# Keys of the second cross attention turned once: a store on GpSimd in the first one, two steps moved to ScalarE in the second

## The chip, the core and the metric

The kernel runs on one core of a Trainium2 chip. TensorE multiplies and transposes (a transpose is a product with the identity), VectorE and ScalarE work elementwise from PSUM and SBUF, GpSimd from SBUF alone, and SyncE issues transfers between DRAM and SBUF. GpSimd can issue transfers too. The engines run their own instruction streams and wait for one another on semaphores. The metric is the device time of one execution in microseconds (us), lower is better.

## The reference, cut to what matters

A block of two layers on `x` (16 batches, 64 tokens, 512 features). Each layer is cross attention to a context of 16 x 512 x 512, then a second attention or time mixing, then a feed forward network. Both layers attend to the same context:

```python
x = x + _L0_xattn_ref(_layernorm(x), ctx_1024, ctx_1024, mask, Wq, bq, Wk, bk, Wv, bv, Wo, bo)
...
x = x + _L1_xattn_ref(_layernorm(x), ctx_1024, ctx_1024)
...
def _L1_xattn_ref(query, key, value):          # 16 heads of 32 features, 512 keys
    scores = jnp.einsum('bhqd,bhkd->bhqk', Q, K) / jnp.sqrt(32)
    weights = jax.nn.softmax(scores, axis=-1)
    out = jnp.einsum('bhqk,bhkd->bhqd', weights, V)
```

The first one projects keys and values from the context; the second takes the context as it is. The last feed forward network rounds its weights to three values: `round(w * scale)` clipped to -1 and 1.

## The kernel before, in words

The whole block is one program of stages with barriers between them: layer norm, projected cross attention (`projected_attention`, names `l0x_`), time mixing, a network with 4-bit weights, layer norm, `ternary_means`, the second cross attention (`cross_attention`, names `l1x_`), sparse attention, the ternary network. In each stage every engine has a written-out instruction list; nothing else orders the work.

**First cross attention.** It goes over pairs of batches, 8 steps a pair (4 a batch). For each batch the context (512 keys by 512 features) is loaded and its four feature chunks are turned on TensorE (`turn`, L460), one chunk a step, two batches ahead. A turned chunk is split into an upper and a lower part, so that projections in the faster format lose nothing: VectorE masks the bits into `l0x_upper` (L697) and subtracts (L700, into `l0x_ctxT_lower`), ScalarE copies the upper part into `l0x_ctxT` (L617) and counts `ctxt_ready`. Both are double buffered by batch. TensorE projects with three products a chunk (L478), in two work banks by turns: before it reuses a bank it waits until this bank's last content was copied away, by ScalarE for keys (L621), by VectorE for values (L687, `l0x_V`). VectorE also masks scores (L709), quantises weights of a later stage (L156 to L173, five operations a step in six of eight steps), and sums magnitudes of the ternary weights (L756, and L759, a sum of two 128x1 operands in SBUF). GpSimd subtracts for two weights (L449) and adds the bias row to eight tiles of `X` (L453), and is then done.

**Second cross attention.** 64 steps `k`, four a batch; a step covers two pairs of heads. TensorE's list in a step: turn two probability tiles (L943), in step 2 turn the finished heads of the batch before (L970), scores for step k + 2 (L932), in steps 0 and 2 a half product of probabilities and context (L959), and turn one context chunk for five steps ahead (`turn`, L919). The keys `l1x_KT` are these turned chunks, copied by ScalarE (`key_copy`, L1000) into two buffers. VectorE takes maxima of the scores (L1043) and copies turned probabilities from PSUM (L1071); ScalarE takes exponentials (L1006), copies one of the eight probability tiles of a batch (in step 3, L1026) and the heads (L1012). The first turn of a step waits for the first exponential and for the copy that empties its bank, the second turn for the second ones.

Beside it the ternary weights are rounded in 24 pieces of 128x1024, three a pair of batches, by three passes on GpSimd: scale and add a large number (L886), clip (L889), subtract the number and write bfloat16 (L893). SyncE waits for the third pass, stores the piece and loads the next one, then loads a context once a half product has released its buffer. SyncE's list is in order, so a wait holds what stands behind it.

## Time and profile before

| | us |
|---|---|
| median of 3 runs (1753.8 to 1759.28) | 1757.63 |
| the profiled execution | 1758.54 |
| its span | 1756.8 |

| engine | busy us | share of the span |
|---|---|---|
| TensorE, matmuls | 1528.7 | 87% |
| VectorE | 1122.2 | 64% |
| ScalarE | 591.7 | 34% |
| GpSimd | 295.8 | 17% |

The first cross attention lies at about 51 to 664 us of the span, the second at 1254 to 1461. In the rows below a line of the timeline is start, duration, engine, source line, operation, output and inputs, count; in brackets the idle time of the engine ahead of it and who ended it. PE is TensorE, PEld its weight loads, DVE VectorE, ACT ScalarE, POOL GpSimd, SPq SyncE's queue. The duration of a line with a count spans all of them. Ends of matmuls are modelled; starts are better taken from one line to the next.

### The profile page before, as it was taken

To read this page: it belongs to the slowest core of one execution; us is meant where nothing else is said; L and a number is where in the kernel's file an instruction comes from. 1 tells how busy PE (TensorE), PEld (TensorE's weight loads), DVE (VectorE), ACT (ScalarE), POOL (GpSimd) and SP (SyncE) were. 2 spreads that over 40 slices of the span, in tenths; PEclk is the share of its full clock that TensorE was granted. 3 is DMA by queue.
4 is the path that set the end of the run, shared out by engine and by line. 5 is a ranking of instruction groups with operands and counts; after the bars stand their busy time and mean duration, and the time that the engine had idled before them with its cause. 6 is when DMAs were issued, how large, how long until landed. Compare 5 with 4: busy or idle time off the path is not lost. (4 is left out here: it accounts for less than half of the span.)

```text
span 1756.8 us, 34069 instructions
## 1 busy us (share of the span) xinstructions
PE 1528.7 (87%) x14116; PEld 996.4 (57%) x14130; DVE 1122.2 (64%) x2155; ACT 591.7 (34%) x1221; POOL 295.8 (17%) x185
## 2 busy tenths in 40 slices
PE   6789999999999994998577899998799995895786
PEld 3567777777777763344545344444466663585343
DVE  3257667676676765521975757675488883765575
ACT  1244443443434442132023110111466662044332
POOL 0400000000000000310010000000499992160000
PEclk9889999999999997899888899998899997998899
DMA  6113122231222204000005000000455421004001
GB/s 231 61 39 132 64 84 86 75 126 70 83 80 90 75 19 158 0 0 1 4 2 198 1 0 0 0 0 0 186 178 191 169 99 35 1 3 145 0 0 48
DMA packets 47909, 120.05 MB, mean 68 GB/s; under 512 B 10605, under 2 KB 15469, under 8 KB 43674
## 3 DMA queue, kind: packets, MB, share of 16 engines
q1 hardware_dynamic: 47770, 118.04, 19.6%
q8 instruction: 107, 1.75, 0.4%
q14 instruction: 32, 0.26, 0.0%
HBM read 100.95 MB, written 17.07 MB: 67 GB/s over the span
## 5 line engine op out<-in xcount | busy, mean ns | idle before, releaser
L1130 POOL TENSOR_TENSOR tm_mixed<-tm_mixed,XNT 128x512 f32<-128x512 f32 x16 | 21.8, 1382 | 662.1 <-DVE tm_mixed L1153 662.1
L617 ACT ACTIVATE l0x_ctxT<-l0x_upper 128x512 fp32r<-128x512 f32 x64 | 40.4, 631 | 237.4 <-DVE l0x_ctxT_lower L700 237.4
L478 PE MATMUL bank<-l0x_ctxT,l0x_upper_k 128*128 128x512 f32 x256 | 104.7, 409 | 5.1 <-ACT l0x_upper_k L627 5.1
L697 DVE TENSOR_SCALAR l0x_upper<-bank 128x512 int32<-128x512 int32 x64 | 44.0, 688 | 95.2 <-PE bank L460 90.6
L478 PE MATMUL bank<-l0x_upper_v,l0x_ctxT 128*128 128x512 f32 x256 | 102.6, 401 | 0.0
L478 PE MATMUL bank<-l0x_ctxT,l0x_lower_k 128*128 128x512 f32 x256 | 101.5, 396 | 0.0
L478 PE MATMUL bank<-l0x_ctxT_lower,l0x_upper_k 128*128 128x512 f32 x256 | 101.4, 396 | 0.0
L478 PE MATMUL bank<-l0x_upper_v,l0x_ctxT_lower 128*128 128x512 f32 x256 | 100.6, 393 | 0.0
L478 PE MATMUL bank<-l0x_lower_v,l0x_ctxT 128*128 128x512 f32 x256 | 100.5, 392 | 0.0
L709 DVE CUSTOM_DVE_ANT_0 l0x_prob<-bank,l0x_mask 128x512 f32<-128x512 f32 x128 | 83.1, 687 | 21.2 <-PE bank L489 20.9
L1043 DVE TENSOR_REDUCE l1x_negmax<-bank 128x1 f32<-128x512 f32 x128 | 82.4, 686 | 21.2 <-PE bank L932 20.8
L635 ACT ACTIVATE l0x_prob<-l0x_prob,l0x_negmax 128x512 f32<-128x512 f32 x128 | 91.3, 720 | 3.3 <-DVE l0x_negmax L709 3.3
L687 DVE TENSOR_TENSOR l0x_V<-bank,rows 128x512 f32<-128x512 f32 x64 | 44.1, 689 | 71.7 <-PE bank L478 70.7
L889 POOL TENSOR_SCALAR l1x_piece<-l1x_piece 128x1024 f32<-128x1024 f32 x24 | 87.2, 3634 | 2.0
L1006 ACT ACTIVATE l1x_prob<-bank,l1x_negmax 128x512 f32<-128x512 f32 x128 | 87.1, 689 | 1.3 <-DVE l1x_negmax L1043 1.3
L245 PE MATMUL bank<-ident,XN 128*128 128x128 f32 x192 | 34.4, 363 | 56.4 <-DVE XN L225 56.4
L1627 PE MATMUL bank<-f_gateT,f_x 128*128 128x512 f32 (+1 forms) x192 | 82.3, 572 | 1.4 <-ACT f_x L1665 1.4
L1071 DVE COPY l1x_PT<-bank 128x512 f32<-128x512 f32 x112 | 72.8, 685 | 12.5 <-PE bank L943 12.5
L669 ACT ACTIVATE l0x_PT<-bank 128x512 f32<-128x512 f32 x128 | 69.5, 592 | 33.2 <-PE bank L587 32.1
L1673 ACT ACTIVATE f_silu<-bank 128x512 f32<-128x512 f32 (+1 forms) x24 | 13.5, 562 | 196.7 <-PE bank L1627 196.7
L1651 PE MATMUL bank<-f_downT,f_hT 128*128 128x512 f32 x176 | 78.6, 603 | 1.2 <-ACT f_hT L1683 1.2
L1627 PE MATMUL bank<-f_upT,f_x 128*128 128x512 f32 (+1 forms) x192 | 79.5, 557 | 0.0
(264 smaller groups left out, 3373.5 us busy)
## 6 DMA issues: line engine op xcount, KB each, us to landing
l0x_ctx<-in_ctx SPq DMA_DIRECT2D x16, 1024.0 KB, 5.3
l1x_ctx<-in_ctx SPq DMA_DIRECT2D x16, 1024.0 KB, 5.8
fp_weight<-l0x_weight_piece SPq DMA_DIRECT2D x24, 352.0 KB, 2.4
f_raw<-fp_weight SPq DMA_DIRECT2D x3, 2816.0 KB, 17.4
ternary_weight<-l1x_piece_out SPq DMA_DIRECT2D x24, 256.0 KB, 6.1
f_raw<-ternary_weight SPq DMA_DIRECT2D x3, 2048.0 KB, 14.1
l0x_abs_piece<-in_L_ffn_w_gate SPq DMA_DIRECT2D x8, 512.0 KB, 5.7
l0x_mask<-mask_scratch SPq DMA_DIRECT2D x16, 256.0 KB, 3.6
```

The lines of the kernel that those rows point to most:

```text
L478: last = nc.tensor.matmul(work[bank][:, :], stationary, moving, start=kc == 0 and i == 0, stop=kc == CH - 1 and i == 2)
L635: nc.scalar.activation(prob[:, :], prob[:, :], ACT.Exp, scale=-1.0, bias=w.negmax[:, p:p + 1], accum_out=w.rowsum[:, par, p:p + 1]).then_i ...
L669: nc.scalar.activation(w.PT[r][:, :], probt[i][:, :], ACT.Copy).then_inc(probt_ready, 1)
L687: nc.vector.tensor_tensor(w.V[par][:, p - CH, :], work[bank][:, :], g.rows[:, 0, :], ALU.add).then_inc(value_ready, 1)
L697: nc.vector.tensor_scalar(upper.bitcast(I32), work[bank][:, :].bitcast(I32), UPPER_BITS, None, ALU.bitwise_and).then_inc(ctx_upper, 1)
L709: nc.vector.tensor_tensor_reduce(w.prob[2 * (s % 2) + i][:, :], score[i][:, :], w.mask[par][:, :], 1.0, 3e38, ALU.add, ALU.min, w.negmax[: ...
L889: nc.gpsimd.tensor_scalar(part, part, WHOLE - 1, WHOLE + 1, ALU.max, ALU.min).then_inc(piece_step, 1)
L1006: nc.scalar.activation(w.prob[2 * (k % 2) + i][:, :], score[2 * (k % 2) + i][:, :], ACT.Exp, bias=w.negmax[:, p:p + 1], accum_out=w.rowsum ...
L1043: nc.vector.tensor_reduce(w.negmax[:, p:p + 1], score[2 * (k % 2) + i][:, :], AX.X, ALU.max, negate=True).then_inc(max_ready, 1)
L1071: nc.vector.tensor_copy(w.PT[2 * s + i][:, :], probt[i][:, :]).then_inc(probt_ready[i], 1)
L1627: last = nc.tensor.matmul(bank[:, 0:n], w.x[:, kc, :], weight[:, kc, at:at + n], start=kc == 0, stop=kc == CH - 1)
L1651: ins = nc.tensor.matmul(work[1][:, :], w.hT[:, kc * P:(kc + 1) * P], w.downT[:, kc, :], start=kc == 0, stop=kc == IC0 - 1)
```

## The change

- In the first cross attention GpSimd adds the upper and the lower part of each turned chunk into one buffer `l0x_whole` and stores it (256 KB) to a new DRAM tensor `turned_context`, 64 times, issuing the stores itself and waiting for each before the next addition. VectorE waits, ahead of splitting a chunk into a buffer in use, for the sum of the chunk that was there 8 chunks ago (`whole_ready`). The bias additions stand between the chunks of each pair of batches.
- In the second cross attention TensorE turns no context and ScalarE copies no keys. SyncE loads the keys, 1 MB a batch, into three buffers `l1x_KT` (three of them ahead of the stage, among the context loads), each released by the last scores of its batch.
- The third rounding pass is done by ScalarE (`whole_weights`, with a constant of minus the large number as bias), in steps 2 and 3 of a batch.
- ScalarE copies one probability tile in step 1 too; VectorE one less.

```diff
@@ projected_attention, gpsimd
+            def store_contexts(b):
+                for c in range(CH):
+                    n = b * CH + c
+                    pool.wait_ge(ctxt_ready, n + 1)
+                    if n > 0:
+                        pool.wait_ge(whole_stored, 16 * n)
+                    nc.gpsimd.tensor_tensor(w.whole[:, :], w.ctxT[b % 2][:, c, :].bitcast(F32),
+                                            w.ctxT_lower[b % 2][:, c, :].bitcast(F32), ALU.add).then_inc(whole_ready, 1)
+                    pool.wait_ge(whole_ready, n + 1)
+                    nc.gpsimd.dma_start(d.ctxT[b, :, c, :], w.whole[:, :]).then_inc(whole_stored, 16)
...
                 nc.gpsimd.tensor_tensor(g.X[:, t, :], g.X[:, t, :], g.rows[:, 1, :], ALU.add).then_inc(bias_added, 1)
+                store_contexts(2 * t)
+                store_contexts(2 * t + 1)
+            pool.wait_ge(whole_stored, 16 * B * CH)
@@ vector, context_parts
+                if count > 2 * CH:
+
+                    dve.wait_ge(whole_ready, count - 2 * CH)
@@ cross_attention, sync
+                if b + 3 < B:
+                    sp.wait_ge(score_full, DOUBLES * (b + 1))
+                    sp.dma_start(w.KT[b % 3][:, :, :], d.ctxT[b + 3]).then_inc(keys_loaded[b % 3], 16)
@@ gpsimd, rounding
-                nc.gpsimd.tensor_scalar(w.piece_out[k][:, :], part, WHOLE, None, ALU.subtract).then_inc(piece_done, 1)
@@ tensor
-                if k + AHEAD < B * CH:
-                    turn(k + AHEAD)
@@ scalar
+            def whole_weights(b, k):
+                turn = b // 4
+                act.wait_ge(piece_step, (turn * 6 + k) * 2 + 2)
...
+                nc.scalar.activation(w.piece_out[k][:, :], w.piece[k][:, :], ACT.Identity,
+                                     bias=w.minus_whole[:, :]).then_inc(piece_done, 1)
...
-                if s == 3:
+                if s % 2 == 1:
                     act.wait_ge(probt_full[1], k + 1)
                     if b > 0:
-                        act.wait_ge(half_full, 2 * b)
+                        act.wait_ge(half_full, 2 * b + s // 2 - 1)
                     nc.scalar.activation(w.PT[2 * s + 1][:, :], probt[1][:, :], ACT.Copy).then_inc(probt_ready[1], 1)
                 if k + 1 < STEPS:
                     exponential(k + 1, 1)
-                if k + AHEAD < B * CH:
-                    key_copy(k + AHEAD)
...
+                if s >= 2 and s - 2 < len(PIECES_OF[b % 4]):
+                    whole_weights(b, PIECES_OF[b % 4][s - 2])
@@ vector
-                for i in range(1 if s == 3 else 2):
+                for i in range(1 if s % 2 == 1 else 2):
```

TensorE in the second cross attention, steps 0 to 2 of the first batch, before (`l1x_ctx` is the context, `l1x_prob` a probability tile):

```order
L943 MATMUL bank<-ident,l1x_prob_10781 128x128 x4
L943 MATMUL bank<-ident,l1x_prob_10782 128x128 x4
L932 MATMUL bank<-l1x_KT_10775,XNT 64x512 x4
L919 MATMUL bank<-ident,l1x_ctx_10778 128x128 x4
L943 MATMUL bank<-ident,l1x_prob_10783 128x128 x4
L943 MATMUL bank<-ident,l1x_prob_10784 128x128 x4
L932 MATMUL bank<-l1x_KT_10775,XNT 64x512 x4
L919 MATMUL bank<-ident,l1x_ctx_10778 128x128 x4
```

and the same place now:

```order
L942 MATMUL bank<-ident,l1x_prob_11160 128x128 x4
L942 MATMUL bank<-ident,l1x_prob_11161 128x128 x4
L931 MATMUL bank<-l1x_KT_11152,XNT 64x512 x4
L942 MATMUL bank<-ident,l1x_prob_11162 128x128 x4
L942 MATMUL bank<-ident,l1x_prob_11163 128x128 x4
L931 MATMUL bank<-l1x_KT_11152,XNT 64x512 x4
```

The turns of the context are gone, and scores are followed by the next turn of probabilities directly.

ScalarE in the second cross attention, steps 2 and 3 of the first batch, before (`l1x_PT` is a turned probability tile):

```order
L1006 ACTIVATE l1x_prob_10783,l1x_rowsum<-bank,l1x_negmax 128x512
L1006 ACTIVATE l1x_prob_10784,l1x_rowsum<-bank,l1x_negmax 128x512
L1000 ACTIVATE l1x_KT_10776<-bank 128x512
L1006 ACTIVATE l1x_prob_10781,l1x_rowsum<-bank,l1x_negmax 128x512
L1026 ACTIVATE l1x_PT_10792<-bank 128x512
L1006 ACTIVATE l1x_prob_10782,l1x_rowsum<-bank,l1x_negmax 128x512
L1000 ACTIVATE l1x_KT_10775<-bank 128x512
```

and steps 2 and 3 of the second batch now:

```order
L1007 ACTIVATE l1x_prob_11162,l1x_rowsum<-bank,l1x_negmax 128x512
L1007 ACTIVATE l1x_prob_11163,l1x_rowsum<-bank,l1x_negmax 128x512
L1000 ACTIVATE l1x_piece_out_11187<-l1x_piece_11181,l1x_minus_whole 128x1024
L1007 ACTIVATE l1x_prob_11160,l1x_rowsum<-bank,l1x_negmax 128x512
L1025 ACTIVATE l1x_PT_11171<-bank 128x512
L1007 ACTIVATE l1x_prob_11161,l1x_rowsum<-bank,l1x_negmax 128x512
L1000 ACTIVATE l1x_piece_out_11188<-l1x_piece_11182,l1x_minus_whole 128x1024
```

Passes of 1024 columns stand where key copies of 512 stood; a batch has one or two of them in place of four key copies.

GpSimd in the first cross attention now, behind its two subtractions (before, eight bias additions stood in a row and nothing behind them):

```order
L464 TENSOR_TENSOR X<-X,rows 128x512
L452 TENSOR_TENSOR l0x_whole<-l0x_ctxT_84,l0x_ctxT_lower_105 128x512
L455 DMA turned_context<-l0x_whole 128x512
L452 TENSOR_TENSOR l0x_whole<-l0x_ctxT_84,l0x_ctxT_lower_105 128x512
L455 DMA turned_context<-l0x_whole 128x512
```

Addition and store alternate, eight of each behind every bias addition.

## Rows read from the trace of the kernel before

**Rows 1.** Windows: a stretch of either stage; busy (count) by engine, PEclk, DMA share, GB/s

```profile
400.00:500.00 100.00, 98.56 (x820) 74.34 (x819) 69.06 (x137) 40.56 (x87) 0.00 (x0) 1.00 0.22 71
...
1275.50:1448.10 172.60, 172.55 (x2940) 112.56 (x2936) 146.95 (x253) 118.98 (x310) 168.73 (x71) 1.00 0.47 162
```

**Rows 2.** Timeline, TensorE, one step of the second cross attention

```profile
1276.26 1.10 PE L959 MATMUL bank<-l1x_PT,l1x_ctx 128*32 128x64 f32 x64
1277.29 0.66 PE L919 MATMUL bank<-ident,l1x_ctx 128*128 128x128 f32 x4
1277.78 1.04 PE L943 MATMUL bank<-ident,l1x_prob 128*128 128x128 f32 x8
1278.75 1.09 PE L932 MATMUL bank<-l1x_KT,XNT 32*64 32x512 f32 x8
```

**Rows 3.** Timeline, TensorE, half products 14 batches apart

```profile
1270.27 1.10 PE L959 MATMUL bank<-l1x_PT,l1x_ctx 128*32 128x64 f32 x64
...
1442.80 1.10 PE L959 MATMUL bank<-l1x_PT,l1x_ctx 128*32 128x64 f32 x64
```

**Rows 4.** Timeline, the last steps of the stage, which have no turn of context

```profile
1449.68 1.09 PE L943 MATMUL bank<-ident,l1x_prob 128*128 128x128 f32 x8
...
1450.70 1.09 PE L932 MATMUL bank<-l1x_KT,XNT 32*64 32x512 f32 x8
...
1451.72 1.09 PE L943 MATMUL bank<-ident,l1x_prob 128*128 128x128 f32 x8
1451.86 1.29 DVE L1043 TENSOR_REDUCE l1x_negmax<-bank 128x1 f32<-128x512 f32 x2 [0.20 <-PE bank L932]
...
1452.59 0.69 ACT L1006 ACTIVATE l1x_prob<-bank,l1x_negmax 128x512 f32<-128x512 f32 x1 [1.05 <-DVE l1x_negmax L1043]
```

**Rows 5.** Timeline, VectorE from the maxima of step 1 to those of step 2

```profile
1353.84 1.29 DVE L1043 TENSOR_REDUCE l1x_negmax<-bank 128x1 f32<-128x512 f32 x2 [0.20 <-PE bank L932]
...
1357.48 1.29 DVE L1043 TENSOR_REDUCE l1x_negmax<-bank 128x1 f32<-128x512 f32 x2
```

**Rows 6.** Timeline, the copy between two exponentials, and TensorE's wait behind it

```profile
1445.73 0.60 ACT L1026 ACTIVATE l1x_PT<-bank 128x512 f32<-128x512 f32 x1
1446.20 0.70 ACT L1006 ACTIVATE l1x_prob<-bank,l1x_negmax 128x512 f32<-128x512 f32 x1
...
1447.04 0.42 PEld L943 LDWEIGHTS bank<-ident,l1x_prob 128*128 128x128 f32 x4 [0.27 <-ACT l1x_prob L1006]
```

**Rows 7.** Groups by line: ScalarE's copy of 128x1024; busy us, mean ns, idle before

```profile
L2207 ACT ACTIVATE f_hT<-bank 128x1024 bf16<-128x1024 bf16 x16 | 15.5, 1021 | 5.1 <-PE bank L2173 5.1
```

**Rows 8.** Timeline, TensorE at the start of the second cross attention

```profile
1254.48 2.37 PE L919 MATMUL bank<-ident,l1x_ctx 128*128 128x128 f32 x20 [0.73 <-PEq L2002]
```

**Rows 9.** Timeline, time mixing: VectorE additions without and with GpSimd's beside them

```profile
714.58 0.69 DVE L1160 TENSOR_TENSOR tm_mixed<-tm_mixed,XNT 128x512 f32<-128x512 f32 x1
...
716.67 2.94 POOL L1130 TENSOR_TENSOR tm_mixed<-tm_mixed,XNT 128x512 f32<-128x512 f32 x2 [640.59 <-DVE tm_mixed L1153]
717.17 1.32 DVE L1160 TENSOR_TENSOR tm_mixed<-tm_mixed,XNT 128x512 f32<-128x512 f32 x1
```

**Rows 10.** Bias additions; ScalarE's chunk copies (ns, starts); a store's landing, 1444 to 1462

```profile
66.03 10.04 POOL L453 TENSOR_TENSOR X<-X,rows 128x512 f32<-128x512 f32 x8
...
L617 ACT ACTIVATE l0x_ctxT<-l0x_upper x64: 629/632/634, 53.8 to 610.2; 128x512 fp32r<-128x512 f32 x64
...
ternary_weight<-l1x_piece_out SPq DMA_DIRECT2D x1, 256.0 KB, 4.1
```

**Rows 11.** Timeline, a step of the first cross attention in which TensorE waits

```profile
298.76 0.63 ACT L617 ACTIVATE l0x_ctxT<-l0x_upper 128x512 fp32r<-128x512 f32 x1 [1.20 <-DVE l0x_ctxT_lower L700]
...
299.89 0.16 DVE L759 TENSOR_TENSOR abs_sum<-abs_sum,l0x_abs_part 128x1 f32<-128x1 f32 x1
...
305.01 1.52 DVE L687 TENSOR_TENSOR l0x_V<-bank,rows 128x512 f32<-128x512 f32 x2
...
305.75 0.42 PEld L460 LDWEIGHTS bank<-ident,l0x_ctx 128*128 128x128 f32 x4 [0.37 <-DVE l0x_V L687]
```

More of the change, by code:

```diff
@@ L820, in context_loads @@
     for b in range(len(w.ctx)):
+        if b < 3:
+            sp.dma_start(w.KT[b][:, :, :], d.ctxT[b]).then_inc(w.keys_loaded[b], 16)
         sp.dma_start(w.ctx[b][:, :, :], context(d)[b]).then_inc(w.ctx_loaded[b], 16)
@@ L850, in cross_attention @@
     ctx_dram = context(d)
-    AHEAD = CH + 1
-    turn_bank = [work, pv, probt[0], probt[1]]
-    def chunk_bank(j):
-        return turn_bank[j] if j < CH else work
     with nc.Block() as block:
@@ L889, in rounding @@
                 nc.gpsimd.tensor_scalar(part, part, WHOLE - 1, WHOLE + 1, ALU.max, ALU.min).then_inc(piece_step, 1)
-                pool.wait_ge(piece_step, before + 2)
-                if turn > 0:
-                    pool.wait_ge(piece_stored[k], 16 * turn)
-                nc.gpsimd.tensor_scalar(w.piece_out[k][:, :], part, WHOLE, None, ALU.subtract).then_inc(piece_done, 1)
             def add_heads(t):
@@ L908, in _ @@
         def _(pe):
-            def turn(j):
-                b, c = j // CH, j % CH
-                if c == 0:
-                    pe.wait_ge(ctx_loaded[b % 4], 16 * (b // 4 + 1))
-                if j >= CH:
-                    pe.wait_ge(key_ready, 1 if j == CH else j)
-                if (j - AHEAD) % DOUBLES == 2 and j > AHEAD + DOUBLES:
-                    pe.wait_ge(heads_done, (j - AHEAD) // DOUBLES)
-                for kc in range(KC):
-                    last = nc.tensor.transpose(chunk_bank(j)[:, kc * P:(kc + 1) * P], w.ctx[b % 4][:, kc, c * P:(c + 1) * P],
-                                               g.ident[:, :])
-                last.then_inc(ctx_turned, 1)
             def scores(k):
@@ L926, in scores @@
                 half = s // 2
-                pe.wait_ge(key_ready, b * CH + 2 * half + 2)
+                if s == 0:
+                    pe.wait_ge(keys_loaded[b % 3], 16 * (b // 3 + 1))
                 for e in range(2):
@@ L932, in scores @@
                         last = nc.tensor.matmul(score[2 * (k % 2) + i][e * T:(e + 1) * T, :], w.QT[rows, c, b * T:(b + 1) * T],
-                                                w.KT[b % 2][rows, c, :], start=True, stop=True)
+                                                w.KT[b % 3][rows, c, :], start=True, stop=True)
                 last.then_inc(score_full, 1)
@@ L972, in turn_back @@
                 last.then_inc(heads_back, 1)
-            for j in range(AHEAD):
-                turn(j)
             for k in range(2):
                 scores(k)
-            pe.wait_ge(key_ready, CH)
             for k in range(STEPS):
@@ L985, in _ @@
                     scores(k + 2)
+                if s == 0:
+                    pe.wait_ge(ctx_loaded[b % 4], 16 * (b // 4 + 1))
                 if s == 2:
@@ L1012, in heads_copy @@
                 nc.scalar.activation(w.headsT[b % 2][:, :], pv[:, 0:256], ACT.Copy).then_inc(heads_out, 1)
-            for j in range(AHEAD):
-                key_copy(j)
             for i in range(2):
@@ L2308, in projected_attention_buffers @@
         w.headsT = a("l0x_headsT", [P, CH, P], F32)
+        w.whole = a("l0x_whole", [P, KEYS], F32)
         w.Wq, w.Wk, w.Wv, w.Wo = (a(f"l0x_{n}", [P, CH, D], F32) for n in ('Wq', 'Wk', 'Wv', 'Wo'))
@@ L2338, in attention_buffers @@
         w.QT = g.XNT
-        w.KT = [a(f"l1x_KT{i}", [P, CH, KEYS], F32) for i in range(2)]
+        w.KT = [a(f"l1x_KT{i}", [P, CH, KEYS], F32) for i in range(3)]
+        w.minus_whole = a("l1x_minus_whole", [P, 1], F32)
         w.ctx = [a(f"l1x_ctx{i}", [P, KC, D], F32) for i in range(4)]
@@ L2349, in attention_buffers @@
         w.piece_out = [a(f"l1x_piece_out{i}", [P, ABS_PIECE], BF16, 2) for i in range(6)]
-        w.ctx_loaded, w.piece_loaded = take("ctx_loaded", 4), take("piece_loaded", 6)
+        w.ctx_loaded, w.piece_loaded, w.keys_loaded = take("ctx_loaded", 4), take("piece_loaded", 6), take("keys_loaded", 3)
         return w
```

19 lines of the change are left out of this document (11 added, 8 removed).

## The prediction, made before the run

> **What bounds the kernel now.** I read the busy table by stage first, then the merged timeline of each stage that the change touches, then the groups by line. Both touched stages are bound by TensorE: in the first cross attention it is busy 98.56 of 100 us, with VectorE at 69 and GpSimd at 0; in the steady part of the second it is busy 172.55 of 172.60 us at full clock, with GpSimd at 168.73, VectorE at 146.95 and ScalarE at 118.98 [rows 1]. So what counts is what TensorE loses in the second stage, which engine is next when it does, and what new work on GpSimd does to TensorE in the first stage.
>
> A busy figure of matmuls is modelled, so I take intervals from one start to the next. In a step of the second stage (two pairs of heads; four steps are a batch) the turn of a context chunk takes 0.49, the turn of the probabilities 0.97, a half product, in every second step, 1.03 [rows 2], and the scores 1.02 [rows 4]. From the half product at 1270.27 to the one at 1442.80 there are 14 batches, so a batch takes 12.32 [rows 3]. Four times 2.48 and twice 1.03 leave 0.34, the turn of the finished heads, which is one more short operation of each batch: there is no gap, and TensorE sets the pace.
>
> **The change part by part, second stage.** The change takes out all 64 turns (59 of them between the steps, 5 ahead of them) and the 64 ScalarE key copies. The price of a step without a turn is in the trace, since the last steps of the stage have none: probabilities at 1449.68, scores at 1450.70, probabilities at 1451.72, so 2.04 in place of 2.48 [rows 4]. A turn is thus worth 0.44, not 0.49. The floor of a batch is 4 x 2.04 + 2 x 1.03 + 0.34 = 10.56, a gain of 1.76.
>
> What is late next? I walk one batch, counted from the start of TensorE's step 0, with scores of step 1 at 4.09 (2.04 + 1.03 + 1.02). VectorE can start the maxima 1.16 after the scores start (1450.70 to 1451.86) [rows 4], at 5.25. From there its work of steps 1, 2 and 3 runs without a break: maxima, two copies, reciprocal and heads take 3.64 from 1353.84 to 1357.48 [rows 5], so the next maxima start at 8.89, and take 1.29 until 10.18. Then comes the one copy of step 3 that is left to it, about 0.69, to 10.87. The next batch's first turn of probabilities would like to start at 10.56 and needs the bank that this copy empties: 0.3 late. ScalarE is a little later. Its first exponential for that turn starts 0.73 after the maxima (1451.86 to 1452.59) [rows 4], at 9.62; then, by the new order, the probability copy at 10.31, the second exponential 0.47 behind it at 10.78, and TensorE's second half 0.84 behind that (1446.20 to 1447.04), at 11.62 [rows 6]. The second half begins 0.5 after the first, so the batch turns over at about 11.1. The trace has that very wait once already, 0.27 at 1447.04, where the turn is gone and the copy stands between the exponentials [rows 6].
>
> I take 11.1 a batch, with 10.56 and 12.3 as ends: 14 x (12.32 - 11.1) = **17.1 less**.
>
> The third rounding pass moves from GpSimd to ScalarE, 24 times. For 128x1024 to bfloat16 ScalarE's nearest row is 1.02 [rows 7]. In step 2 it runs from 7.3 to 8.3 in my walk, before the exponential at 9.62 can start: hidden, with 1.3 to spare. In every second batch one more runs in step 3, from 11.5 to 12.5; the exponential behind it then starts 0.8 late, but TensorE wants it only at 14.2 and has it by 14.0: just hidden. If that cover goes, it costs up to 1.5 x 1.02 a batch. GpSimd drops from 98% busy to some 60%, and would otherwise be the bound: its work of 168.73 us in those 172.60 would hold a batch near 12.0. With the pass gone it runs ahead and nobody waits for it, except that the queue of SyncE now waits for ScalarE's pass before it stores a piece.
>
> The one more probability copy (step 1) is 0.60 on ScalarE instead of 0.68 on VectorE; it is in the walk. The key loads are 16 transfers of 1 MB. They stand in SyncE's queue behind the wait for the piece's pass and ahead of the context load; they are issued in step 3 of a batch and wanted in step 2 two batches on, about 19 us, against 5 to 8 that a 1 MB transfer takes. The transfers moved 162 GB/s at a share of 0.47 [rows 1], so 345 at most; a batch will move 3.3 MB in 11.1 us, 295 GB/s. They fit, with little room.
>
> At the start the five turns ahead of the first scores go, 2.37 of TensorE [rows 8], and three turns ahead of the steady part, 1.3: **3.7 less**. Three more megabytes ahead of the weight pieces bring the first piece to GpSimd some 5 us later; ScalarE asks for it in step 2, by then about ready. The stage's last store is now issued about a microsecond after the last probability copy, while half product, heads and the last addition still follow; it lands up to 4.1 later [rows 10]: nothing, or half a us.
>
> **First stage.** GpSimd gets 64 additions of 128x512 and 64 stores of 256 KB, and waits for each store before the next addition. The addition takes 1.25 alone (10.04 / 8) [rows 10] and 1.47 beside VectorE's (2.94 / 2) [rows 9]. A store issued by GpSimd isn't in the trace; SyncE's of 256 KB into DRAM landed after 4.1 in a quiet stretch [rows 10]. So a chunk takes about 5.7; bounds 3.3 (half the landing) and 9.7 (twice it). Chunks come every (610.2 - 53.8) / 63 = 8.8 us [rows 10], so GpSimd keeps up, and VectorE's new wait (for the sum of 8 chunks ago, ahead of a chunk's splitting) never holds. The Trainium skill, page "DMA: Bandwidth & Descriptors", the anatomy of a GpSimd DMA, gives 2.0 us plus the bytes at 436 GB/s, an estimate of 2.6 us here, by which the cycle would be 4.2; no run here shows it yet, and the sum would be the same.
>
> The additions do touch VectorE. Where a GpSimd addition runs at 716.67, VectorE's addition of two SBUF tensors takes 1.32 in place of 0.69, and GpSimd's two take 2.94 in place of 2.5 [rows 9]: one waits for the other. The Trainium skill, page "SBUF — State Buffer", section "Who interferes with whom", says just that: the pair of ports is locked for a whole instruction when a VectorE instruction with two SBUF inputs meets a GpSimd one that reads SBUF. The trace agrees, and the rule speaks against this change.
>
> Where does it reach TensorE? In one place of each pair of batches. At 299.4, when the chunk is ready (298.76 + 0.63), GpSimd's addition would start and run to 300.8; VectorE's tiny sum of two SBUF operands at 299.89 waits for it, 0.9, and all behind it shifts, down to the value copy at 305.01, for which TensorE already waits at 305.75 [rows 11]. So 0.9 goes straight to TensorE, in 7 such places: **6.3 more**. In the other steps the value copy behind the rounding steps has 1.5 us of room, more than the 0.9. Bounds: 0, if so small an operation slips through, and 22, if all 24 runs of rounding steps that meet an addition reached TensorE.
>
> **Sum.** 1758.54 - 17.1 - 3.7 + 6.3 = 1744.0. The profiled execution is 0.9 above the median of the three runs, so 1743.
>
> **The rivals.**
> (a) TensorE's floor and a free lock: the chain of exponentials costs nothing and the additions hide: -14 x 1.76 - 3.7 = -28.3, 1729. For it: 1451.72 starts on time. Against it: the wait at 1447.04.
> (b) ScalarE becomes the bound: half of the passes fall on its chain, 1.5 x 1.02 / 2 = 0.8 a batch, 11.9: -5.9 - 3.7 + 6.3, 1754. For it: the walk has only 0.2 of room in every second batch. Against it: ScalarE has 54 us idle in the 172.60.
> (c) The other side: GpSimd's chain of addition, issue and landing sets the pace of the first stage. VectorE's split of chunk 64 waits for sum 56; GpSimd starts at 67.3, behind one bias addition (66.03 + 10.04 / 8) [rows 10], and that split starts at 608.8 (two VectorE operations of 0.7 ahead of the last ScalarE copy of a chunk, at 610.2 [rows 10]), so it decides from (608.8 - 67.3) / 56 = 9.7 us a chunk on, and each us above costs 56. At 10.5 it is 47 more, 1790. Against it: 5.7 by the nearest rows.
> (d) The change doesn't give what it says: the doubled context traffic binds. Reads and writes mixed at 265 GB/s instead of 345 would hold a batch at 12.3, and only the start's 3.7 and the lock's 6.3 stay: 1760.
>
> **How the numbers follow.** Forecast 0.64, (a) 0.12, (b) 0.13, (c) 0.06, (d) 0.05. The range from 1729 to 1755 holds all of the forecast's own spread (10.8 to 11.5 a batch, 0 to 8 in the first stage: 1734 to 1750), (a) and half of (b). A measurement of this kernel can tell about 0.3%, 5.3 us, from no change. Faster than 1752.4: all but 0.02 of the forecast, (a), and 0.07 of (b), 0.81. Within: 0.11, from the rests of these and (d). Slower: (c) and 0.02 of the rest, 0.08.
>
> **What would show it.** Half products 11.1 apart per batch, with TensorE's waits, if any, on the exponentials in step 0's second half; VectorE over 90% busy; the second stage 21 us shorter. If the interval is 10.6, (a) holds; if TensorE's waits end on an exponential behind a pass, (b). In the first stage the tiny sum near a 0.9 longer or idle ahead of it, and the wait of TensorE for the value copy 1.2 instead of 0.37, once in each pair of batches; GpSimd's additions one for each chunk, right behind ScalarE's copy. A VectorE wait on GpSimd ahead of a split would be (c); a TensorE wait on a key load (d). I would be wrong most of all if the long first stage, which I read in one pair of batches, pays for GpSimd in more places than the one.

## The result, and the profile after

The changed kernel takes 1746.17 us (median of 6 runs, 1744.31 to 1751.94), the kernel before in runs beside it 1756.70 (6 runs, 1753.8 to 1759.28). The ratio is 0.9944, with a 95% interval of 0.9926 to 0.9962: 0.4 to 0.7% faster. The forecast was 1743, from 1729 to 1755. The profiled execution took 1744.45, its span is 1742.4 against 1756.8 before.

The layer norms are good marks between stages (VectorE's first operation of each, L215; the first row of all is L278 in the first stage). They divide the 14.4 us between the two traces:

| stretch | before | after | difference |
|---|---|---|---|
| start to L278 | 26.12 | 25.77 | -0.35 |
| first cross attention | 654.06 | 659.96 | **+5.90** |
| time mixing | 255.38 | 253.25 | -2.13 |
| 4-bit network | 304.05 | 303.43 | -0.62 |
| second cross attention with its layer norm | 222.04 | 204.21 | **-17.83** |
| sparse attention | 133.00 | 132.80 | -0.20 |
| ternary network, to its last addition | 152.73 | 153.53 | +0.80 |

**The second stage.** The windows of [rows 1], and from one half product to the one 14 batches on, for the changed kernel (busy us and count of TensorE, its weight loads, VectorE, ScalarE, GpSimd; granted clock, DMA share, GB/s):

```profile
400.00:500.00 100.00, 98.25 (x826) 73.55 (x824) 72.81 (x138) 42.38 (x90) 21.94 (x23) 1.00 0.31 100
1271.36:1427.78 156.42, 150.52 (x2721) 89.44 (x2717) 135.52 (x235) 118.56 (x287) 114.87 (x51) 0.99 0.74 266
```

TensorE is no longer busy all the time: 6 of 156 us are idle. The half products themselves, against [rows 3]:

```profile
1271.36 1.94 PE L958 MATMUL bank<-l1x_PT,l1x_ctx 128*32 128x64 f32 x64
...
1427.78 1.10 PE L958 MATMUL bank<-l1x_PT,l1x_ctx 128*32 128x64 f32 x64
```

14 batches in 156.42, 11.17 each, where it was 12.32: 16.1 us less. Where TensorE waits now is the same place in every batch, the turn of probabilities in step 0. Timeline, changed kernel, from the finished heads to that turn:

```profile
1338.85 0.20 DVE L1049 RECIPROCAL l1x_rinv<-l1x_rowsum 128x8 f32<-128x8 f32 x1
1339.08 0.86 DVE L1056 TENSOR_TENSOR l1x_heads<-bank,l1x_rinv 64x256 f32<-64x256 f32 x2
...
1339.97 1.29 DVE L1042 TENSOR_REDUCE l1x_negmax<-bank 128x1 f32<-128x512 f32 x2
...
1340.70 0.69 ACT L1007 ACTIVATE l1x_prob<-bank,l1x_negmax 128x512 f32<-128x512 f32 x1 [1.16 <-DVE l1x_negmax L1042]
1341.18 0.68 DVE L1070 COPY l1x_PT<-bank 128x512 f32<-128x512 f32 x1
...
1341.37 0.59 ACT L1025 ACTIVATE l1x_PT<-bank 128x512 f32<-128x512 f32 x1
...
1341.85 0.69 ACT L1007 ACTIVATE l1x_prob<-bank,l1x_negmax 128x512 f32<-128x512 f32 x1
1341.97 0.42 PEld L942 LDWEIGHTS bank<-ident,l1x_prob 128*128 128x128 f32 x4 [1.26 <-ACT l1x_prob L1007]
1342.00 1.34 PE L942 MATMUL bank<-ident,l1x_prob 128*128 128x128 f32 x8 [0.41 <-DVE l1x_PT L1070]
...
1342.68 0.42 PEld L942 LDWEIGHTS bank<-ident,l1x_prob 128*128 128x128 f32 x4 [0.29 <-ACT l1x_prob L1007]
```

VectorE goes without a break through heads, maxima and copy; the exponential waits 1.16 for the maxima; TensorE's matmuls wait 0.41 for the copy of 1341.18, and its second weight load 0.29 for the second exponential. The waits for the copy, added up from 1275 to 1440, are 5.6 us in 14 times, once a batch.

**The start of that stage** gave less than it should: the first half product comes 28.95 after the layer norm's first operation instead of 30.66, 1.7 less. In 5 us windows:

```profile
1255.00:1260.00 5.00, 1.58 (x19) 0.65 (x20) 1.97 (x5) 2.77 (x6) 0.24 (x2) 0.99 1.00 423
1260.00:1265.00 5.00, 5.00 (x22) 3.06 (x23) 3.36 (x6) 2.28 (x7) 0.46 (x1) 0.50 1.01 414
1265.00:1270.00 5.00, 5.00 (x24) 2.48 (x26) 3.07 (x6) 3.23 (x10) 4.82 (x3) 0.50 0.81 329
1270.00:1275.00 5.00, 5.00 (x88) 2.87 (x80) 2.22 (x4) 2.20 (x5) 4.82 (x3) 0.65 0.64 174
```

For 13.7 us, to 1273.5, TensorE is granted 0.50 of its clock, 1.2 of 2.4 GHz. In the kernel before the first three of these windows were:

```profile
1255.00:1260.00 5.00, 2.96 (x34) 1.94 (x33) 2.06 (x4) 4.83 (x9) 4.83 (x3) 1.00 0.77 311
1260.00:1265.00 5.00, 5.00 (x24) 2.87 (x25) 3.10 (x5) 2.22 (x7) 4.92 (x3) 0.56 0.36 107
1265.00:1270.00 5.00, 5.00 (x34) 2.66 (x32) 3.44 (x6) 3.03 (x9) 4.92 (x3) 0.76 0.13 52
```

There the clock stood at half for 6.8 us (windows of 1 us), and TensorE had been busy 2.96 instead of 1.58 in the first window.

**The first stage.** GpSimd's addition beside the tiny sum of [rows 11], and the value copy for which TensorE waits, in the changed kernel:

```profile
300.21 1.21 DVE L773 TENSOR_REDUCE l0x_abs_part<-l0x_abs_piece 128x1 f32<-128x1024 f32 x1
300.32 0.63 ACT L631 ACTIVATE l0x_ctxT<-l0x_upper 128x512 fp32r<-128x512 f32 x1 [1.20 <-DVE l0x_ctxT_lower L717]
...
301.04 1.28 POOL L452 TENSOR_TENSOR l0x_whole<-l0x_ctxT,l0x_ctxT_lower 128x512 f32<-128x512 f32 x1 [5.82 <-ACT l0x_ctxT L631]
301.45 0.90 DVE L776 TENSOR_TENSOR abs_sum<-abs_sum,l0x_abs_part 128x1 f32<-128x1 f32 x1
...
308.01 0.42 PEld L474 LDWEIGHTS bank<-ident,l0x_ctx 128*128 128x128 f32 x4 [1.07 <-DVE l0x_V L701]
```

The sum takes 0.90 instead of 0.16, until GpSimd's addition is done (301.04 + 1.28 = 302.32), and TensorE waits 1.07 instead of 0.37. This is not the only sum that meets an addition. All 24 of them (ns, least, median, most):

```profile
L776 DVE TENSOR_TENSOR abs_sum<-abs_sum,l0x_abs_part x24: 158/897/902, 153.0 to 677.2; 128x1 f32<-128x1 f32 x24
```

14 take 0.90, six 0.45 and one 0.22, three in each of seven pairs of batches, and only the last three take 0.16. But in a pair only the one above is followed by a longer wait of TensorE. All 64 additions and stores of GpSimd: durations in ns (least, median, most), who ended its idle time, and the time from a store's issue to its landing:

```profile
L452 POOL TENSOR_TENSOR l0x_whole<-l0x_ctxT,l0x_ctxT_lower x64: 1255/1282/1298, 66.9 to 615.9; 128x512 f32<-128x512 f32 x64
...
  ACT l0x_ctxT L631: 391.1, 57
  DMA turned_context<-l0x_whole: 12.2, 6
```

```profile
L455 POOL DMA_DIRECT2D turned_context<-l0x_whole x64: 557/557/777, 68.5 to 617.4; - x64
...
DMA to landing us min/median/max: 2.3/2.6/7.2
```

It waited for its own stores 6 times, all at the stage's start (71 to 103), where chunks already stand ready; VectorE never waited for `whole_ready`.

### The profile page after: what moved, and what is told of

Read it like the earlier page. It is cut to its first block and busy times, and to the rows that moved or that the text cites. A ratio compares the mean times of both kernels' runs of the same rounds, so it can differ in the third digit from the quotient of the medians.

```text
span 1742.4 us, 33686 instructions
## 1 busy us (share of the span) xinstructions
PE 1505.4 (86%) x13860; PEld 973.0 (56%) x13874; DVE 1127.2 (65%) x2139; ACT 592.8 (34%) x1197; POOL 349.0 (20%) x290
## 5 line engine op out<-in xcount | busy, mean ns | idle before, releaser
L452 POOL TENSOR_TENSOR l0x_whole<-l0x_ctxT,l0x_ctxT_lower 128x512 f32<-128x512 f32 x64 | 81.9, 1279 | 403.3 <-ACT l0x_ctxT L631 391.1
L942 PE MATMUL bank<-ident,l1x_prob 128*128 128x128 f32 x512 | 75.4, 288 | 7.9 <-DVE l1x_PT L1070 5.6
L942 PEld LDWEIGHTS bank<-ident,l1x_prob 128*128 128x128 f32 x512 | 56.8, 144 | 43.3 <-ACT l1x_prob L1007 38.0
```

Source lines behind the costliest of these rows:

```text
L452: nc.gpsimd.tensor_tensor(w.whole[:, :], w.ctxT[b % 2][:, c, :].bitcast(F32), w.ctxT_lower[b % 2][:, c, :].bitcast(F32), ALU.add).then_inc ...
L942: last = nc.tensor.transpose(probt[i][:, kc * P:(kc + 1) * P], w.prob[2 * (k % 2) + i][:, kc * P:(kc + 1) * P], g.ident[:, :])
```

## The experiments

Two theories come out of this. **Chain**: the second stage is held by VectorE's chain of heads, maxima and copy. **Port**, in the first stage: GpSimd's addition holds up the small VectorE sum of two SBUF operands, and so TensorE. Each has rivals in the expectations below. The runs of the kernel before that stood beside each had medians of 1756.3 to 1758.3; ratios are against those.

**The second stage's part alone.**

```diff
-                store_contexts(2 * t)
-                store_contexts(2 * t + 1)
...
-                if count > 2 * CH:
-                    dve.wait_ge(whole_ready, count - 2 * CH)
...
-            sp.dma_start(w.KT[b][:, :, :], d.ctxT[b]).then_inc(w.keys_loaded[b], 16)
+            sp.dma_start(w.KT[b][:, :, :], context(d)[b]).then_inc(w.keys_loaded[b], 16)
```

> The changed kernel without its part in the first cross attention: no additions and no stores of the turned context, no VectorE wait for them. The second one loads its keys from the context as it is given, not turned, at the same times and in the same sizes, so this leaves out the turning of the keys and computes something else. My theory (TensorE's turns gone in the second stage, VectorE's port lock in the first): the layer norm behind the first stage starts at 680.2 as before (685.7 in the changed kernel), the second stage with its layer norm is 204 against 222, half products 11.2 apart; total some 18 to 20 below the kernel before, 1738. Rival, by which the doubled context traffic or the layout of the turned copy costs the second stage part of its gain: no difference in the second stage from the changed kernel would speak against it only for the layout; an interval well under 11.1 for it.

1741.48 us, ratio 0.9909 (0.9890 to 0.9929), 16.8 below the kernel before instead of 18 to 20. First stage 653.88, second with its layer norm 204.39 (changed kernel: 204.21), half products 11.17 apart (1391.42 to 1402.59). The doubled reads stay in this run, and that they come from a copy written by GpSimd costs nothing.

**The first stage's part alone, and its two halves.** To the kernel before were added, in the first run, both of these and VectorE's wait; in the second all but the store; in the third all but the addition and VectorE's wait.

```diff
+                    nc.gpsimd.tensor_tensor(w.whole[:, :], w.ctxT[b % 2][:, c, :].bitcast(F32),
+                                            w.ctxT_lower[b % 2][:, c, :].bitcast(F32), ALU.add).then_inc(whole_ready, 1)
...
+                    nc.gpsimd.dma_start(d.ctxT[b, :, c, :], w.whole[:, :]).then_inc(whole_stored, 16)
```

> The kernel before with the first part alone: GpSimd's 64 additions and 64 stores, and VectorE's wait for them; nothing reads what is stored. If the costs add up: 5.5 to 6 us longer than the kernel before in the first cross attention, nothing behind it. The second cross attention stays at 12.3 a batch. Rival (the cost of 5.5 in the changed kernel is something of the changed layout or of the loads, not of GpSimd's work): under 1.5 more.

1762.95 us, ratio 1.0031 (1.0018 to 1.0043), 3 to 8 us slower. First stage 659.67, +5.6. So the two parts of the change add up: the product of their ratios is 0.9940, the whole change's is 0.9944. In this one trace the second stage, in which nothing is edited, took 1.9 more than in the kernel before (223.91); its start stood at half clock for longer, see the busy start below.

> The kernel before with GpSimd's 64 additions and VectorE's wait for them, without the stores. Port theory: the whole cost is the addition's, the layer norm behind the stage starts 5.5 to 6 us later than before, and the tiny sum takes 0.90 where an addition runs, VectorE's value copy comes late and TensorE's waits for it are about 1.1 each. Rival (the stores, their issue on GpSimd and their traffic of 16.8 MB beside the context loads): within 1 us of the kernel before.

> The kernel before with GpSimd's 64 stores of 256 KB, each of a buffer that is set to zero once, issued when a chunk is turned and after the store before it; no additions, no VectorE wait. It leaves out what the stores should hold. Port theory: within 1 us of the kernel before in the first stage, the tiny sum stays at 0.16. Rival (the stores cost): up to 5.5 more.

One execution of each. First stage with additions alone 657.93, +3.9; with stores alone 653.97, -0.1. TensorE's waits for the value copy in 120 to 600 us (us, times, longest) are those of the changed kernel in the first, and no more than those of the kernel before (2.6, 7, 0.4) in the second. Additions alone, weight loads and matmuls:

```profile
PE bank L471 <- DVE l0x_V L698: 3.8, 6, 0.6
PEld bank L471 <- DVE l0x_V L698: 6.3, 6, 1.1
```

Stores alone:

```profile
PEld bank L474 <- DVE l0x_V L701: 2.2, 6, 0.4
```

The addition makes the waits, the stores don't. The stores' mark was missed in one point: the tiny sum does not stay at 0.16 there.

```profile
L773 DVE TENSOR_TENSOR abs_sum<-abs_sum,l0x_abs_part x24: 158/159/1248, 152.9 to 672.3; 128x1 f32<-128x1 f32 x24
```

Six of the 24 take 1.02 to 1.25, because the stores have moved GpSimd's bias additions beside them (one from 170.47 to 171.77, the sum from 170.55 to 171.79). That is the longest stretch of all, in a place that TensorE doesn't wait behind, and the stage got no longer. So it is the place of the sum that costs, not the stretch.

The 1.7 us between 657.93 and 659.67, additions without and with stores, are not explained by these waits, and two single executions don't show them to be an effect: six traces with the same first stage (with additions, stores and sum) took 657.64 to 659.96.

**Without the tiny sum**, in the changed kernel and, as a control, in the kernel before:

```diff
-                nc.vector.tensor_reduce(w.abs_part[:, i:i + 1], w.abs_piece[:, :], AX.X, ALU.add,
+                nc.vector.tensor_reduce(w.abs_part[:, at:at + 1], w.abs_piece[:, :], AX.X, ALU.add,
                                         apply_absolute_value=True).then_inc(abs_step, 1)
-                dve.wait_ge(abs_step, it * 6 + (2 * i + 1))
-                nc.vector.tensor_tensor(g.abs_sum[:, i:i + 1], g.abs_sum[:, i:i + 1], w.abs_part[:, i:i + 1],
-                                        ALU.add).then_inc(abs_step, 1)
```

> The changed kernel without the 128x1 sums of two SBUF operands in the first cross attention: every reduction writes a column of its own and one reduction adds them up at the end; the result is the same sum. Port theory as I wrote it (GpSimd's addition holds that tiny sum 0.7 to 0.9, and everything behind it on VectorE comes late): the first stage gives back 5 to 6 us, the layer norm behind it starts at 680 to 681, total about 1741. Rival: the lock just catches the next VectorE operation of two SBUF inputs, so that only 0.16 a sum and under 1.5 us in all come back.

> Control for the run before it: the same edit on the kernel before, in which GpSimd has no additions there. Port theory: the tiny sum costs 0.16 and nothing waits for it, 0 to 1.5 us faster than the kernel before. Rival (the tiny sum's chain costs by itself, with or without GpSimd): as much as in the run before it, 5.

In the changed kernel: 1736.40 us, ratio 0.9896 (0.9882 to 0.9911); first stage 650.29, 9.7 less, more than the whole lock had cost. In the kernel before: 1755.37, ratio 0.9989 (0.9980 to 0.9998); first stage 650.81, 3.3 less. The control explains the surplus: the sum cost something without GpSimd too, since with it TensorE waited 0.37 once in each pair of batches already [rows 11]. In both kernels TensorE's wait for the value copy ahead of the chunk's turn is gone (its wait ahead of the output projection, 4.2 us in 12 times, stands in all of them), and both take the same 650 to 651 us. So the additions cost nothing any more when that one small operation is gone. How much of the gain was the lock is known to a microsecond or two: 9.7 - 3.3 = 6.4 by these traces of single executions, 0.66 in each of seven pairs, 4.6, by the pairs (below). By the medians the control gained only 0.9, within the 0 to 1.5 expected. The edit also drops two semaphore waits of VectorE around the sum and lets the next piece of weights load earlier; that these play no part was not tested by itself. The rival, by which the lock would catch the next VectorE operation of two SBUF inputs at the same price, falls. Timeline of the changed kernel without the sum, where GpSimd's addition now meets a masking of scores, which reads PSUM and takes its usual time (0.68 to 0.69 over all 128, before and here):

```profile
294.69 1.28 POOL L452 TENSOR_TENSOR l0x_whole<-l0x_ctxT,l0x_ctxT_lower 128x512 f32<-128x512 f32 x1 [5.82 <-ACT l0x_ctxT L631]
294.98 0.68 DVE L726 CUSTOM_DVE_ANT_0 l0x_prob<-bank,l0x_mask 128x512 f32<-128x512 f32 x1
```

**Heads in step 3**, in the changed kernel:

```diff
-                if s == 2 and b > 0:
+                if s == 3 and b > 0:
                     finish_heads(b - 1)
```

> The changed kernel with one thing moved in the second cross attention: VectorE finishes the heads of the batch before (reciprocal and heads, some 1.1 us) in step 3 in place of step 2. My theory: the wait of 0.4 to 0.6 in each batch is VectorE's chain of maxima, copies, reciprocal and heads in steps 1 to 3, from which the maxima and with them both exponentials of step 3 come late. Then the interval goes from 11.17 to 10.6 a batch and the total is about 8 below the changed kernel, 1738. Rival 1: ScalarE's probability copy between the two exponentials sets the wait; then it keeps 0.3 to 0.5 a batch and the gain is 2 us at most. Rival 2, the other side: the finished heads are what the next half waits for, the interval grows.

1734.09 us, ratio 0.9884 (0.9865 to 0.9903); second stage 194.57, 9.6 less. Windows, from one half product to one 13 batches on:

```profile
1287.92:1424.35 136.43, 136.43 (x2527) 82.26 (x2523) 125.88 (x222) 112.18 (x268) 100.21 (x46) 1.00 0.76 280
```

136.43 / 13 = 10.49 a batch, and TensorE is busy every microsecond. ScalarE's copy still stands between the two exponentials, and costs nothing: rival 1 falls, what held the batch was when VectorE's maxima of step 3 began.

**One copy back**, in the changed kernel:

```diff
-                if s % 2 == 1:
+                if s == 3:
                     act.wait_ge(probt_full[1], k + 1)
...
-                for i in range(1 if s % 2 == 1 else 2):
+                for i in range(1 if s == 3 else 2):
```

> The changed kernel with one part undone: the second probability copy of step 1 is VectorE's again. Theory (VectorE's chain of maxima, copies and heads sets the batch): that chain is longer by one copy of 0.69, the interval goes from 11.17 to 11.8 or 11.9, the stage is some 9 to 10 longer, total about 1755. Rival (ScalarE's order of copy and exponentials sets it): ScalarE has 0.6 less to do, the interval is the same or shorter.

1744.53 us, ratio 0.9922 (0.9907 to 0.9937), the changed kernel's 0.9944 (0.9926 to 0.9962) overlaps it; second stage 204.44, half products 11.17 apart. My expectation was wrong, and against my own walk: the chain begins with the maxima behind step 1's copies, and these have room ahead of it. Timeline of this run, VectorE:

```profile
1344.31 1.29 DVE L1070 COPY l1x_PT<-bank 128x512 f32<-128x512 f32 x2 [0.30 <-PE bank L942]
...
1345.80 1.29 DVE L1042 TENSOR_REDUCE l1x_negmax<-bank 128x1 f32<-128x512 f32 x2 [0.20 <-PE bank L931]
```

With both copies on it, VectorE still idles 0.20 ahead of the maxima (0.79 in the changed kernel). Moving that copy to ScalarE, a named part of the change, is worth nothing here.

**Third pass back on GpSimd**, in the changed kernel:

```diff
+                nc.gpsimd.tensor_scalar(w.piece_out[k][:, :], part, WHOLE, None, ALU.subtract).then_inc(piece_done, 1)
...
-                if s >= 2 and s - 2 < len(PIECES_OF[b % 4]):
-                    whole_weights(b, PIECES_OF[b % 4][s - 2])
```

> The changed kernel with the third rounding pass back on GpSimd. If GpSimd is the next bound behind TensorE, as the prediction says: its 168.7 us of work in 14 batches set 12.0 a batch, 0.9 more than the changed kernel's 11.17, or about 12 us on the stage, so that of the 16 us won only 4 are left; TensorE waits on heads for GpSimd, or the context for a piece. Rival (GpSimd's backlog is taken up by the buffers, nobody waits for it): within 2 us of the changed kernel.

One execution, 1755.11; second stage 217.27, 13.1 more. The size was right, the place wrong: half products are still 11.17 apart (1422.69 to 1433.86), nobody waits for GpSimd on the way. It is busy 137.11 of 140 us and falls behind, and the debt is paid at the end, where the last half product is long done (1441.45):

```profile
1444.84 2.78 POOL L909 TENSOR_SCALAR l1x_piece_out<-l1x_piece 128x1024 bf16<-128x1024 f32 x1
1447.60 1.12 POOL L902 TENSOR_SCALAR l1x_piece<-l1x_piece,inv_mean 128x1024 f32<-128x1024 f32 x1
...
1452.51 2.78 POOL L909 TENSOR_SCALAR l1x_piece_out<-l1x_piece 128x1024 bf16<-128x1024 f32 x1
1455.26 2.48 POOL L914 TENSOR_TENSOR X<-X,l1x_heads 128x512 f32<-128x512 f32 x2
...
1458.80 1.29 DVE L215 BATCH_NORM_STATS2 stats<-X 128x6 f32<-128x512 f32 x2 [14.34 <-PEq L76]
```

**Both repairs**, heads in step 3 and no tiny sum:

> The changed kernel with both edits that the two theories led to: finished heads in step 3 of the second stage, and no 128x1 sums in the first. They act in different stages, so their gains in the traces (9.6 and 9.7 us) should add: second stage with its layer norm 195, the layer norm behind the first stage at 674 to 676, total 1744.5 - 19.3 = 1725 in the trace of one execution, 30 below the kernel before. Rival (the gain of one stage is given back behind it, by transfers or the clock): 1732 or more.

1731.66 us, ratio 0.9863 (0.9844 to 0.9882); first stage 651.08, second 194.69: in their stages the gains add, 8.9 and 9.5. The total is 14.5 below the changed kernel by the medians, 14.9 in the spans (1727.5), not 19.3: in this execution time mixing took 255.06 instead of 253.25 and sparse attention 133.78 instead of 132.80, which are edited in neither. The two stages themselves gave 18.4 instead of 19.3 (the median, next to the rival's 1732, doesn't tell the theories apart), and the 4-bit network (303.96), the start and the last stage took the remaining 0.7.

**A busy start**, first on top of both repairs, then on the changed kernel alone:

```diff
+            def idle_turns(count):
+                for i in range(count):
+                    nc.tensor.transpose(work[:, 0:P], g.ident[:, :], g.ident[:, :])
+
+            idle_turns(4)
             for k in range(2):
                 scores(k)
+            idle_turns(13)
```

> The run before it with 17 more turns of the identity on TensorE at the start of the second cross attention, 4 ahead of the first scores and 13 behind them, whose result nobody reads: the idle time there (0.73 and 1.58 us) is filled. In the kernel before, with 20 turns there, the granted clock of TensorE was back at full 8 us after it fell at 1260, in the changed kernel 13 us after. Theory: that is why the start gave 1.7 us in place of the 3.7 forecast; with TensorE busy the clock comes back some 5 us earlier and the stage is 1 to 2.5 us shorter, less 0.5 for the turns themselves. Rival (the clock falls and rises by something else, or the transfers hold the start): no gain, or 0.5 lost.

> The changed kernel with nothing but the 17 more turns of the identity at the start of the second cross attention. With the run before it that had them on top of two other edits, the first half product came 24.8 instead of 29.0 after the start of the layer norm, but the granted clock fell later on, and 1.3 us of the stage was left, while the median of the whole kernel was 5.4 lower. If the turns do only what the trace of their stage shows: that stage with its layer norm is 203 against 204.2, and the median 1 to 2 below the changed kernel's 1746. Rival (they also change what follows, by the clock or the transfers): 4 or more below, with the stages behind shorter too.

On top of both: 1726.30 us, ratio 0.9818 (0.9801 to 0.9834), the best version found, 31 us below the kernel before. Alone: 1741.85, ratio 0.9913 (0.9899 to 0.9926). Alone, the second stage takes 201.09, 3.1 less than in the changed kernel, and the first half product comes 26.71 after the layer norm's start, not 28.95. Its windows beside those of the changed kernel above:

```profile
1255.00:1260.00 5.00, 3.10 (x22) 1.18 (x22) 0.34 (x2) 1.93 (x3) 0.24 (x2) 0.75 1.02 429
1260.00:1265.00 5.00, 5.00 (x45) 3.69 (x37) 4.52 (x8) 2.90 (x9) 0.85 (x1) 0.91 1.02 413
1265.00:1270.00 5.00, 4.88 (x94) 2.68 (x93) 4.75 (x8) 4.26 (x10) 4.82 (x3) 1.00 0.68 275
```

The clock fell here too, to half, but from 1257.5 to 1260.9 only (windows of 1 us): 3.4 us in place of 13.7. The other traces say that this isn't one execution's chance. From the layer norm's start plus 14 us on, the clock stood at half for 13.6 or 13.7 us in six traces without any turns there, and for 17.1 in the seventh (the changed kernel without the tiny sum); for 6.8 in four traces with TensorE's list of the kernel before and for 10.3 in the fifth (the first stage's part alone); for 3.4 in this one with the 17 turns, and not at all up to the first half product in the other. Two executions against seven: the turns shorten it, but a busy figure of the window ahead doesn't say when the clock falls: it was 2.96 of 5 in the kernel before and 3.10 here. The two marks "8 us" and "13 us" of the expectation are 6.8 and 13.7.

The transfers were as dense (413 to 429 GB/s), so they did not hold TensorE's start. They do hold the first piece of the ternary weights: GpSimd gets it 22.1 after the layer norm's start, in the changed kernel (1264.55) as on top of both repairs (1253.52). There the first half product came 24.79 after the layer norm's start instead of 29.02, and ScalarE asked for that piece too early. Timeline, on top of both repairs:

```profile
1258.38 1.15 ACT L1006 ACTIVATE l1x_piece_out<-l1x_piece,l1x_minus_whole 128x1024 bf16<-128x1024 f32 x1 [2.29 <-POOL l1x_piece L904]
...
1260.25 0.66 PE L941 MATMUL bank<-ident,l1x_prob 128*128 128x128 f32 x4 [0.91 <-ACT l1x_prob L1013]
```

The pass stands ahead of the exponentials in ScalarE's list, so TensorE idled 0.91 and then 0.50, and behind that the clock fell to half for 3.4 us (0.75 from 1260 to 1265). Of the 4.2 won at the start the stage kept 1.3 (193.40). A first pass put one batch later would be the next thing to try; it was not run.

Both medians moved by more than their stage, by 5.4 and 4.3 us. Alone, that is as much as the rival asked for, but the stages behind took only 1.2 us less together. Between single executions the start of the whole kernel (23.0 to 26.1 to L278) and time mixing (253.2 to 255.4) differ by 2 to 3 us whatever was edited, and which of that belongs to the edit stays open.

## Why the prediction held, step by step

| term | forecast | measured |
|---|---|---|
| 14 batches of the second stage | -17.1 | -16.1 |
| its start | -3.7 | -1.7 |
| its tail | 0 to +0.5 | 0.0 |
| first stage | +6.3 | +5.9 |
| stretches that the change doesn't touch | 0 | -2.5 |
| sum, in the profiled executions | -14.5 | -14.4 |

The sum is better than its terms. The two terms of the second stage came out 3.0 short, the first stage 0.4 cheaper, and 2.5 us came from stretches without an edit, mostly time mixing, where executions differ by as much anyway. That last row is luck, and it is why 14.5 and 14.4 shouldn't be read as precision. The two edited stages alone gave 11.9, close to what the medians say: they fell by 10.5, to 3 above the forecast. The profiled execution of the changed kernel was the second shortest of its six, that of the kernel before was above its median.

- **What is late next**: right in place and size. The walk said 11.1, by VectorE's chain from the maxima through heads to the copy of step 3, 0.3 late at TensorE's first turn (measured 0.41), with the second exponential a little later (0.29 more at its second half). It left open which of the two the batch hangs on, and put the larger delay on ScalarE; the run with the heads moved showed that both go when VectorE's chain is shortened, down to 10.49, the floor that the prediction gave as 10.56. So rival (a) was one line of code away, but not what this change does.
- **Price of the third pass on ScalarE, rival (b)**: 1.02 by the nearest row, measured 1.14. Hidden, as said: ScalarE idles 1.16 ahead of the exponential that could have been late, and with the pass taken off ScalarE again a batch still takes 11.17. With it (b) falls.
- **The one more copy**: "it is in the walk", the prediction said. It wasn't; in the walk of VectorE from the maxima to the copy of step 3 there is no copy of step 1, and undone it changes nothing.
- **GpSimd as the next bound**: the price (12 forecast, 13.1 measured) was right, "would hold a batch near 12.0" was not. Here, where its products are wanted late, GpSimd didn't slow the pace; its backlog was paid once, at the stage's end. With the pass gone it is busy 114.87 of 156.42, 73%, not some 60%.
- **Start**: the term of 3.7 counted TensorE's instructions at the clock that they had before. Up to the first turn of probabilities 2.8 were won (17.51 after the layer norm's start instead of 20.32); from there to the first half product 1.1 went back (11.44 instead of 10.34, with fewer instructions), at half clock. Taking work from an engine that waits at the stage's start also changed its clock: 13.7 us at half instead of 6.8. With 17 turns that nobody reads, the first half product comes 3.95 earlier than in the kernel before (26.71 instead of 30.66). The first weight piece was "about ready" as said, with 0.4 to spare (1269.38 against 1269.75), and no longer once the start got faster.
- **Key loads, rival (d)**: TensorE never waited for keys. 1 MB landed after 7.3 in the median, as the 5 to 8 assumed; the traffic was 266 GB/s, not 295. "345 at most" was too low a ceiling: the stage's start moved 414 to 429 GB/s, at a share of 1.00 to 1.02.
- **GpSimd's chunk, rival (c)**: forecast 5.7 a chunk (its two rows add up to 5.6); back to back it does one in 4.1 (the addition 1.28, 0.30 up to the issue and a landing of 2.5 from there, in which the 0.56 of the issue itself lie), far from the 9.7 from which it would decide. The Trainium skill, page "DMA: Bandwidth & Descriptors", the anatomy of a GpSimd DMA, was cited with an estimate of 2.6 for the landing and 4.2 for the cycle. The trace agrees with it (2.6 in the median, 4.1), and less well with my nearest row, a landing of 4.1.
- **The lock**: forecast 0.9 in 7 places, 6.3. The tiny sum did take 0.90, but 0.74 more than before, not 0.9, and TensorE's wait grew by 0.70 (0.37 to 1.07): 4.9 in 7 places. The pairs of batches show it directly: over four pairs, from one first addition of VectorE into `X` to another, 74.21 each after (271.38 to 568.24), 73.55 before (269.82 to 564.01), 73.22 in the changed kernel without the sum (265.06 to 557.94). That is 0.66 a pair, 4.6 in seven. The other microsecond wasn't traced to a wait, and is within the 2.3 us by which traces with the same first stage differ; 6.3 against 5.9 is no closer a hit than that. That the long stage would pay in more than one place of a pair, the largest doubt of the prediction, didn't come true: 21 sums were stretched, and the others had the room that it gave them. The Trainium skill, page "SBUF — State Buffer", section "Who interferes with whom", states the lock; the runs show it for an operation of one column.

Of the marks named, two were missed: VectorE is busy 135.52 of 156.42, 87%, not over 90% (only at 10.49 a batch is it 92%), and the second stage is 17.8 shorter, not 21.

## What to carry to other kernels

When the bound engine loses work, walk one period of the others to see what arrives late next, and then look at where each operation of that chain could stand: here a bookkeeping step of 1.1 us, moved by one step, gave 9.6 us in its stage, where the whole change nets 10.5. A GpSimd operation that is off everybody's path can still hold the smallest VectorE operation with two SBUF inputs until its own end; most of these stretches cost nothing, so look for the small ones ahead of whatever the bound engine waits for, and do without them. Work removed from TensorE where it is mostly waiting can be paid for by its clock. And a start that gets faster asks earlier for everything that is loaded for it.

## What the runs showed of the hardware

- A VectorE addition of two 128x1 operands in SBUF takes 0.16 alone; when it starts during GpSimd's addition of 128x512 it lasts until that one's end: 0.22 to 0.90 in 21 places of the changed kernel, 1.02 to 1.25 in six of the run with stores alone. GpSimd's own duration stays 1.26 to 1.30 over all 64. I had left open that so small an operation slips through.
- At the start of the second cross attention TensorE's granted clock stood at 0.50 for 6.8 us (10.3 in one of five traces) with the kernel before's list, for 13.7 (17.1 in one of seven) where 20 turns were taken out of the idle time ahead of the steps, and for 3.4 where 17 turns that nobody reads filled it, with a stage 3.1 us shorter (in the other trace with these turns it fell only later, for 3.4, behind waits of 0.91 and 0.50).
- A 256 KB store issued by GpSimd takes 0.56 of its own time, and landed 2.6 after its issue began in the median (2.3 to 7.2).
